# A Fourier-space block MLP on one core: 64-row and 128-row tiles taken in turn by pairs of column groups

## The reference

```python
xf = jnp.fft.rfft2(x, axes=(1, 2), norm='ortho')        # x: (4, 128, 128, 768) fp32
xf = xf.reshape(B, H, W // 2 + 1, 8, 96); xr, xi = xf.real, xf.imag
o1r = relu(einsum('bhwni,nio->bhwno', xr, w1[0]) - einsum(xi, w1[1]) + b1[0])
o1i = relu(einsum(xi, w1[0]) + einsum(xr, w1[1]) + b1[1])
o2r = einsum(o1r, w2[0]) - einsum(o1i, w2[1]) + b2[0]
o2i = einsum(o1i, w2[0]) + einsum(o1r, w2[1]) + b2[1]
o = softshrink(stack([o2r, o2i]), 0.01)
out = irfft2(complex(o), s=(128, 128), axes=(1, 2), norm='ortho') + x
```

## Time and profile before

| what | value |
|---|---|
| median of 3 runs | 5289.3 us (5289.18 to 5289.44) |
| the profiled execution | 5295.64 us |
| its span | 5293.8 us |
| TensorE, matmuls in flight | 5047.7 us, 95% |
| VectorE busy | 3859.0 us, 73% |
| ScalarE busy | 2978.4 us, 56% |
| GpSimd busy | 1434.6 us, 27% |
| mean granted clock of TensorE, share of full speed | 0.984 |
| DMA queue of the kernel | 422.47 MB, 36.1% of 16 engines |

### The profile page before, as it was taken

The page is one execution under the profiler, slowest core; times in us unless marked ns, Lnnn a source line. Parts: engine busy times, 40 slices in busy tenths (PEclk is TensorE's granted clock), DMA queues, the critical chain, the costliest instruction groups (busy, mean ns, idle before and its releaser), DMA issues.

```text
span 5293.8 us, 113159 instructions
## 1 busy us (share of the span) xinstructions
PE 5047.7 (95%) x40128; PEld 4731.8 (89%) x40128; DVE 3859.0 (73%) x6195; ACT 2978.4 (56%) x5384; POOL 1434.6 (27%) x905
## 2 busy tenths in 40 slices
PE   6999999999999999999999999999999999999997
PEld 5999889998899988999989998999998999988996
DVE  4777777777777777777767777777777777777775
ACT  4555655556555556555565555655556655556553
POOL 3033312333123332233331233312333223332120
PEclk8999999999999999999999999999999999999998
DMA  4034432344323444223443234432334422344322
GB/s 109 16 87 101 101 71 53 80 101 101 82 55 79 89 101 100 54 64 86 101 102 68 57 82 98 101 79 61 76 89 101 95 58 65 86 101 101 71 67 61
DMA packets 1699963, 430.22 MB, mean 81 GB/s; under 512 B 1699104, under 2 KB 1699232, under 8 KB 1699360
## 3 DMA queue, kind: packets, MB, share of 16 engines
q1 hardware_dynamic: 1699360, 422.47, 36.1%
HBM read 220.89 MB, written 201.33 MB: 80 GB/s over the span
## 4 chain that ended last, share of the span: by engine, by line
PE 90%; DVE 6%; issue 2%; ACT 1%; SPq 1%; DMA 0%; DVEq 0%; ACTq 0%
PE psum L768 15%; PE psum L742 14%; PE psum L818 13%; PE psum L791 13%; PE psum L724 10%; PE psum L801 9%; PE psum L754 7%; PE psum L830 3%; PE psum L831 3%; PE psum L832 3%; DVE spectrum L633 1%; DVE spectrum L632 1%; DVE mixed L654 1%; DVE x L691 1%; SPq L361 1%
## 5 line engine op out<-in xcount | busy, mean ns | idle before, releaser
L654 DVE COPY mixed<-psum 128x768 f32<-128x768 f32 (+1 forms) x544 | 508.1, 934 | 838.5 <-PE psum L754 838.5
L742 PE MATMUL psum<-w_whole,whole 128*128 128x192 f32 x4160 | 796.6, 334 | 110.1 <-ACT whole L480 101.5
L544 ACT ACTIVATE sums_high<-psum 128x512 fp32r<-128x512 f32 x768 | 458.9, 597 | 727.2 <-PE psum L818 727.2
L768 PEld LDWEIGHTS psum<-mats,mixed 128*128 128x128 f32 x6272 | 744.0, 191 | 121.2 <-issue 112.0
L768 PE MATMUL psum<-mats,mixed 128*128 128x128 f32 x6272 | 841.8, 283 | 0.0
L742 PEld LDWEIGHTS psum<-w_whole,whole 128*128 128x128 f32 x4160 | 684.2, 200 | 130.9 <-ACT whole L480 107.6
L724 PE MATMUL psum<-mats,x 128*128 128x128 f32 x6144 | 725.3, 280 | 65.3 <-DVE spectrum L633 28.7
L724 PEld LDWEIGHTS psum<-mats,x 128*128 128x128 f32 x6144 | 713.0, 196 | 75.7 <-DVE spectrum L633 28.9
L791 PE MATMUL psum<-w2t,hidden 128*128 128x192 f32 x4160 | 768.2, 327 | 0.0
L818 PE MATMUL psum<-mats,spectrum 128*128 128x128 f32 x6144 | 743.4, 275 | 13.2 <-DVE spectrum L661 13.2
L818 PEld LDWEIGHTS psum<-mats,spectrum 128*128 128x128 f32 x6144 | 714.2, 192 | 15.6 <-DVE spectrum L661 15.6
(11 more groups left out here) (83 smaller groups left out, 7491.9 us busy)
## 6 DMA issues: line engine op xcount, KB each, us to landing
x<-x SPq DMA_DIRECT2D x736, 192.0 KB, 2.8
out<-x SPq DMA_DIRECT2D x736, 192.0 KB, 2.4
x<-x SPq DMA_DIRECT2D x736, 64.0 KB, 2.6
out<-x SPq DMA_DIRECT2D x736, 64.0 KB, 2.2
x<-x SPq DMA_DIRECT2D x32, 144.0 KB, 2.7
w2t<-L_conv_w SPq DMA_DIRECT2D x128, 36.0 KB
out<-x SPq DMA_DIRECT2D x32, 144.0 KB, 2.3
x<-x SPq DMA_DIRECT2D x64, 48.0 KB, 2.2
```

What stands on the lines that cost most here:

```text
L654: dve.tensor_copy(mixed[s % 2][:, 0:k], both_b(s)[:, 0:k]).then_inc(b_copied, 1)
L742: pe.matmul(bank_b(s, k), whole[s % 2][:, k // 2, :, k % 2], w1_whole[par][:, :, :].rearrange("p r o -> p (r o)"), start=k % 2 == 0, stop= ...
L768: last = pe.matmul(out[tile], flat[:, tile * SIZE:(tile + 1) * SIZE], mat(FH), start=True, stop=True)
```

## The change

TensorE's order in the layers is now made of rounds k, each with two groups, odd = 2k-1 and even = 2k. An even group takes its 128-row tiles first and its 64-row tiles last, as before. An odd group takes the 64-row tiles of the first layer first, in the round before, and the 128-row tiles last; so too the second layer. The flags `start` and `stop` of the matmuls, and the place where `b_done` and `d_done` are reported, follow. All 64-row blocks of a round stand together: first layer of 2k, second layer of 2k-2 and of 2k-1, first layer of 2k+1.

ScalarE and VectorE have their lists rewritten to the same rounds. One unfolding step is done per round and no longer one per group. The six negations are ScalarE's now, two in each of rounds 4, 5 and 6; the bias split stays with VectorE, one step at the end of each of these rounds. ScalarE's loop has seven turns and an eighth written out behind it. No arithmetic is added or left out.

```diff
--- before.py
+++ after.py
@@ ScalarE @@
-            def gather(s):
+            def gather_whole(s):
...
+            def gather_halved(s):
...
+            def negate(m, par, k):
+
+                act.wait_ge(w_loaded[par], (m + 1) * W_LOADS * 16)
+                parts = [w1_whole[par][BLOCK:SIZE, 0], w1_halved[par][:, 0]]
+                parts += [w2t[par][lo:hi, col:col + BLOCK] for lo, hi, col in NEGATED]
+                for part in parts[2 * k:2 * k + 2]:
+                    act.activation(part, part, ACT.Copy, scale=-1.0).then_inc(w_negated, 1)
+
+            def layers(m, par, n, last):
...
+                gather_whole(0)
+                act.wait_ge(w_loaded[par], (m + 1) * W_LOADS * 16)
+                gather_halved(1)
+                gather_whole(1)
+                for k in range(NS // 2 + 2):
+                    odd, even = 2 * k + 1, 2 * k + 2
+                    if k > 0 and odd < NS:
+
+                        act.wait_ge(b_done, n * NS + (odd - 1))
+                        gather_whole(odd)
+                    if k > 0:
+                        hide(par, n, even - 4)
+                    if k > 1:
+                        exceed(n, odd - 4)
+                    if k > 0 and odd - 2 < NS:
+                        hide(par, n, odd - 2)
+                    if k > 0 and odd < NS:
+                        gather_halved(odd)
+
+                    if 0 <= k - NS // 4 < W_SIGNS // 2 and not last:
+                        negate(m + par, 1 - par, k - NS // 4)
+                    if even < NS:
+
+                        act.wait_ge(b_done, n * NS + (even - 1))
+                        gather_whole(even)
+                    if k > 0:
+                        exceed(n, even - 4)
+                    if even < NS:
+                        gather_halved(even)
@@ VectorE @@
-            def prepare_step(m, par, k):
+            def split_bias(m, par, k):
...
+            def layers(m, par, n, first, last):
+                mix(n, 0)
+                for k in range(1, NS // 2 + 2):
+                    odd, even = 2 * k - 1, 2 * k
+                    if odd < NS:
+                        mix(n, odd)
+                    hide_middle(par, n, even - 2)
+
+                    if k <= 2 * NP and not first:
+                        unfold_step(n - 1, 1 - par, k - 1)
+                    if k > 1:
+                        shrink(n, odd - 2)
+                    if odd < NS:
+                        hide_middle(par, n, odd)
+                    if 1 < k and odd < NS:
+                        seed(par, n, odd)
+                    if even < NS:
+                        mix(n, even)
+                    shrink(n, even - 2)
+                    if even < NS:
+                        seed(par, n, even)
+
+                    if 0 <= k - NS // 4 < 3 and not last:
+                        split_bias(m + par, 1 - par, k - NS // 4)
@@ TensorE @@
                 for k in columns(s):
-                    pe.matmul(bank_b(s, k), whole[s % 2][:, k // 2, :, k % 2], w1_whole[par][:, :, :].rearrange("p r o -> p (r o)"),
-                              start=k % 2 == 0, stop=False, skip_group_check=True)
+                    last = pe.matmul(bank_b(s, k), whole[s % 2][:, k // 2, :, k % 2], w1_whole[par][:, :, :].rearrange("p r o -> p (r o)"),
+                                     start=s % 2 == 0 and k % 2 == 0, stop=s % 2 == 1, skip_group_check=True)
+                if s % 2 == 1:
+                    last.then_inc(b_done, 1)
...
-                                             start=False, stop=True, skip_group_check=True)
-                last.then_inc(b_done, 1)
+                                             start=s % 2 == 1 and i == 0, stop=s % 2 == 0, skip_group_check=True)
+                if s % 2 == 0:
+                    last.then_inc(b_done, 1)
...
+            def layers(par, n):
+                for k in range(NS // 2 + 2):
+                    odd, even = 2 * k - 1, 2 * k
+
+                    if 0 < odd < NS:
+                        stage_b_whole(par, n, odd)
+                    if k > 0:
+                        stage_c(n, even - 2)
+                    if k > 1:
+                        stage_d_outer(par, n, odd - 2)
+                    if 0 < odd < NS:
+                        stage_c(n, odd)
+                    if k > 0:
+                        if even >= NS:
+                            flip(n)
+                        start_d(n, even - 2)
+                        stage_d_outer(par, n, even - 2)
+                    if odd == 1:
+                        start_d(n, odd)
+                    if even < NS:
+                        stage_b_whole(par, n, even)
+
+                    if even < NS:
+                        stage_b_halved(par, n, even)
+                    if k > 0:
+                        stage_d_middle(par, n, even - 2)
+                    if 0 < odd < NS:
+                        if odd > 1:
+                            start_d(n, odd)
+                        stage_d_middle(par, n, odd)
+                    if odd + 2 < NS:
+                        stage_b_halved(par, n, odd + 2)
```

More of the change, by code:

```diff
@@ L537, in _ @@
[L537 to L544 removed]
+                    forward(n)
+                    layers(m, par, n, last and unit == 2 * UNROLL - 1)
@@ L698, in _ @@
-            for k in range(PREPARE):
-                prepare_step(0, 0, k)
+                    forward(n)
+                    layers(m, par, n, first and unit == 0, last and unit == 2 * UNROLL - 1)
+                    inverse(par, n)
+            for k in range(3):
+                split_bias(0, 0, k)
             turn(0, first=True)
```

319 lines of the change are left out of this document (151 added, 168 removed).

## The result

| | before | after |
|---|---|---|
| median | 5289.2 us (4 runs) | 5441.6 us (4 runs, 5439.9 to 5445.4) |
| ratio, 95% interval | | 1.029 (1.0272 to 1.0308) |
| profiled execution, its span | 5295.6, 5293.8 us | 5445.4, 5442.9 us |
| layers, sum of 32 units | 3083.2 us | 3231.5 us |
| between the layers' stretches, sum of 31 | 2060.1 us | 2061.9 us |

Slower was right, 5344 us was not: the time lies above the range (5285 to 5398). Nearly all that was added is in the layers: 148.3 of the 149.1 us by which the spans differ. All medians here leave out one slow execution, 18143.5 us at a mean granted clock of 0.52, of the kernel of experiment 6.

The account below looks back on a forecast made before the run. TensorE's own list was taken as the bound. 32 x (-0.6) for the order, 30 x 2.0 for weights and 31 x 0.6 for bias gave +60, trimmed to +55: 5344 us, 8-in-10 range 5285 to 5398.

Parts of the forecast that it names:

- part 3: Steady rounds: 10.9 us each if two ScalarE/VectorE chains are in time; both hold, by 0.26 and 0.21 us; nothing charged.
- part 5: Bias-split steps in rounds 5 and 6, between seeding and copy: 0.6 us a unit, at most 1.6 for both; 31 units.
- parts 1 to 3: New order in the layers: fewer borders, new waits at the unit's start, steady rounds uncharged; together -0.6 us a unit.
- part 4: ScalarE's negations wait for late weight transfers in round 4, holding up the next whole tile: 2.0 us a unit, 30 units.
- "few us" taken off: Small deduction from the sum for the last unit and for bias splits that fall short, leaving +55 us.
- Parts 1 and 2: Fewer borders between 128-row and 64-row tiles, -3.6 us a unit; start waits +3.4, old order's wait -0.4.
- part 2: Unit's start: transform of group 1 waits 2.1 us for the Relus, plus three smaller waits; together 3.4 us a unit.
- Rival C: New waits of 2.1 and 2.0 us bring TensorE's clock down in half the units: 5368 to 5392 us; chance 0.08.
- Rival A: Weights come in time, so the negation never waits: 5268 to 5278 us; chance 0.15, with 0.06 for a half-way case.
- B: Chain margins of 0.21 and 0.26 us are absent; each of 7 rounds pays 0.1 to 0.3: 5390 to 5435; chance 0.11.
- D: No borders saved, blocks of different tiles within a visit costing as much as leaving it: 5459 us; chance 0.02.

Follow-up runs that it names:

- experiment 6: Changed kernel with the unfolding done two steps a round in rounds 1 to 4: 5374.3 us, and 5375.2 us in a second series.
- experiment 3: Changed kernel with the three bias steps behind the seeding of the odd group, where VectorE is idle: 5397.7 us.
- Experiment 7: Changed kernel with VectorE copying only the first half of each even group's first-layer sums from group 2 on: 5442.5 us.
- experiments 1 and 4: Two separate edits of the changed kernel: negations two rounds later, 5355.3 us; weight transfers issued ahead of the store of piece 0, 5352.2 us.
- experiment 2: Changed kernel with ScalarE doing group 0's Relu before gathering group 3's whole tile: 5417.2 us.
- experiment 11: Changed kernel with weights issued early, group 0's Relu first, group 2's first layer between the first two transforms, bias steps in rounds 2 to 4: 5240.7 us.
- experiment 5: Kernel before, order untouched, with the six negations moved to ScalarE at the end of its steps 8 to 13: 5286.7 us, ratio 0.9999.

## Why the prediction was wrong

Three steps failed: part 3, which charged nothing for the steady rounds; part 5, which was mis-sized; and the clock, which the sum put at nothing although its own waits bring it down. Us a unit; the measured values are those of the first profile after.

| step | forecast | measured | from |
|---|---|---|---|
| parts 1 to 3, the new order | -0.6 | +0.1 | 95.68 against 95.60 |
| part 4, wait for the weights | +2.0 | +2.2 | mean of round 5 in 30 units, 13.80, less half of its low-clock time, 0.57, less 11.01 |
| part 5, bias steps | +0.6 | +1.5 | mean excess of rounds 6 and 7, 0.48 and 1.02 |
| clock | 0 | +1.0 | 17 us in round 5; at the unit's start 40 us where the kernel before has 24 |

Half of the low-clock time is taken as lost, since TensorE runs at half speed in it. By these rows the layers should be 3 + 66 + 46 + 33 = 148 us longer, and they are 148.3. The forecast's sum was 55 us, the spans differ by 149. Of the 94 missed, about 22 are the order (32 x 0.7), 28 part 5 (31 x 0.9), 33 the clock and 6 part 4; the few left are the "few us" taken off and 2 us outside the layers.

- **Parts 1 and 2.** The borders came down as foretold, weight loads idle on entering are 288 at L814 (its other 32 are the wait in round 1) and 32 at L867, the 320 foretold for 544 and more. The hidden Relu's wait is 1.90 and ends at T0 + 7.0 (4276.46 - 4269.45), for 2.1 and 7.0 worked out.
- **Part 3 failed.** It said "I charge nothing" on two chains with margins of 0.26 and 0.21. These two held, the first with 0.19 (experiment 3). A third chain was overlooked although part 2 had worked it out for round 1: 0.37 + 0.96 + 0.12 = 1.45 us to empty banks 0 and 1, against 1.31 of second-layer blocks between in every full round. Experiment 7 gives it as 0.12 a round. Six rounds have it (2 to 7), so it is 0.7 a unit: what parts 1 to 3 missed by, and more than the 0.6 that the order was to bring.
- **Part 4 was right** in its mechanism, and nearly in its size. ScalarE reaches the wait at T0 + 43.2, as worked out. The landing was put at T0 + 46.4 and is T0 + 46.6 in the unit shown, up to 47.7 in the six units without a fall. (The terms written down for the end of the second unfolding step add up to T0 + 19.2 and not 19.5; the unit shown has 19.3.) There are 30 waits of (158.1 - 45.6) / 30 = 3.75 us, and experiments 1 and 4 take them away from either end. The 20 units whose round 5 has no fall lose 2.0 us there, the forecast's number; but they are those with the shorter waits.
- **Part 5 was mis-sized.** The value was 0.6, the mean is 1.5. The bound of 1.6 holds for the mean and not for each unit: one without a fall has 0.27 + 1.63 = 1.90. The second and third steps have medians of 0.25 and 0.80 us and reach 1.37 and 1.87. A long one is paid in full: what the margin of 0.19 takes is given back by the lost overlap and the longer transform. The late unfolding steps, which the prediction also saw beside the folding, reach 3.27 us and not 1.76, and cost nothing that a round shows.
- **Rival C was no rival.** Its waits were the forecast's own, so it had to be added to it. It was priced about rightly (24 to 48 us; 16 falls at two places, 16 x 1.7 = 27, and 21 falls the second time) and given 0.08. The rest of the clock's loss was in nobody's account: falls at T0 in 23 units and not 16, behind an idle time that is the same before and after, 3.15 us. Why there are more stays open. No row says what part of the clock's loss they are alone, since a fall at T0 shortens the waits of round 1. In the unit with two falls, TensorE waits and then runs at 1.2 GHz, eight passes of the second layer taking 2.5 us to the next block and not 1.3; a granted clock of 0.89 over 14.94 us of round 5 is 3.3 us at the lower level, 1.6 lost:

```profile
4157.17 1.58 PE L829 MATMUL psum<-mats,mixed 128*128 128x128 f32 x12 [2.01 <-DVE middle L680]
4158.58 2.72 PE L855 MATMUL psum<-w2t,hidden 128*128 128x192 f32 x8
4161.09 1.94 PE L798 MATMUL psum<-w_whole,whole 128*128 128x192 f32 x8
```

```profile
4150.94:4165.88 14.94, 12.93 (x90) 12.10 (x88) 8.07 (x10) 10.39 (x21) 0.00 (x0) 0.89 0.92 203
```

The Trainium skill (TensorE: Matmul & The Clock Gate, the table of practical rules under "Why this matters for your kernels") allows gaps up to about 3 us; here falls follow idle times of 1.9 and 2.0 us, so the trace disagrees. None follows the waits of 0.93 us (0 of 32 in experiment 2).
- Rival A is out (the negation waits 30 times), B half true (rounds 2 to 7 pay 0.11 each, but by another chain), D is out (experiment 11).

## What to carry to other kernels

When an order is rewritten, list for each bank or buffer the time to empty it and the work between its two uses, in the steady round as well as at the start: a deficit of 0.14 us there cost 0.7 us a unit, more than the net gain of 0.6 that was forecast. What a forecast takes as a wait of about 2 us has to be priced with the clock that it may bring down. An operation put into a chain with 0.2 us to spare is paid by its length, and that length may be three times as long beside another engine's work; so it goes to where its engine is idle or to before they start.

## What was not expected of the hardware

- An execution has its own number of clock falls: 10 and 13 behind round 5's wait in two profiles of one kernel. At T0, behind the same idle time of 3.15 us, they come in 16 and 8 of 32 units in the old order (before, experiment 5) and in 21 to 28 in eleven profiles of the new order. Medians of kernels that differ by 20 us should be compared by their units without falls.
- A VectorE copy of 192 elements on one partition lasts 0.25 us alone and 1.0 us on average beside GpSimd's folding (experiment 3). In the first profile after, the 15 such copies that no GpSimd instruction overlaps in time last 0.25 us, the other 17 last 0.62 on average; the third step lasts 0.35 (10 times) and 1.22 (22 times). Moved ahead of the folding (experiment 11), the three steps have means of 0.28, 0.26 and 0.40, and the only long ones are in the first unit, beside GpSimd again. The Trainium skill (SBUF — State Buffer, the two separate sides) tells of a port pair locked for a whole instruction, for a VectorE operation with two SBUF inputs or in a two-port mode. The third step has two such inputs, and its rows agree; the copy has one, and no run shows its mode.
